# Weight pieces, loads and row statistics placed elsewhere around the stage boundaries of a two-layer kernel

## What is computed

```python
x = x + tanh(g_xattn[0]) * L0_xattn(layernorm(x), ctx)   # 16 heads of 32, int8-style projections of q and out
x = x + tanh(g_ffn[0])   * L0_ffn(layernorm(x))          # fp4 weights x fp16 group scales, 512-1408-512, silu
x = x + tanh(g_xattn[1]) * L1_xattn(layernorm(x), ctx)   # 16 heads of 128, 4 kv heads, rope, causal plus context
x = x + tanh(g_ffn[1])   * L1_ffn(layernorm(x))          # 64 experts of 512-192-512, top 8, 128 places each
```

## Time and profile before

| | us |
|---|---|
| median of 3 runs (2893.17 to 2900.97) | 2898.32 |
| profiled execution | 2892.45 |
| its span | 2890.7 |
| first attention | 0 to 508 |
| first FFN | 508 to 922 |
| projections | 922 to 1367 |
| second attention | 1367 to 2369 |
| routing | 2369 to 2483 |
| experts and last sum | 2483 to 2891 |

### The profile page before, as it was taken

The page is one execution under the profiler, slowest core; times in us unless marked ns, Lnnn a source line. Parts: engine busy times, 40 slices in busy tenths (PEclk is TensorE's granted clock), DMA queues, the critical chain, the costliest instruction groups (busy, mean ns, idle before and its releaser), DMA issues. The chain is left out here.

```text
span 2890.7 us, 48667 instructions
## 1 busy us (share of the span) xinstructions
PE 2597.6 (90%) x17291; PEld 2097.6 (73%) x17291; DVE 1703.1 (59%) x3806; ACT 1287.4 (45%) x3413; POOL 877.6 (30%) x878
## 2 busy tenths in 40 slices
PE   7899986699998899997999999999999974599895
PEld 5666753699997788885888888888888864355552
DVE  6767677944344766664766666666666656422221
ACT  4777775222223544443655555555555531122121
POOL 3344223200001555553322222222222220244443
PEclk9999998799999999998999999999999985799997
DMA  3110011400013555556412422421331127799976
GB/s 132 48 45 23 20 56 52 126 30 16 30 37 106 181 185 190 191 189 233 140 45 88 142 65 57 144 60 51 92 108 45 38 77 252 217 305 293 298 187 112
DMA packets 227215, 340.07 MB, mean 118 GB/s; under 512 B 24736, under 2 KB 111136, under 8 KB 226464
## 3 DMA queue, kind: packets, MB, share of 16 engines
q1 hardware_dynamic: 209664, 292.78, 31.7%
q0 software_dynamic: 14912, 39.85, 6.7%
q10 hardware_dynamic: 2400, 4.33, 0.5%
HBM read 230.56 MB, written 110.53 MB: 118 GB/s over the span
## 5 line engine op out<-in xcount | busy, mean ns | idle before, releaser
L2019 POOL TENSOR_SCALAR a_prob<-a_prob,a_rinv 128x640 f32<-128x640 f32 (+3 forms) x256 | 252.4, 986 | 756.9 <-DVE a_rinv L2180 756.9
L2170 DVE TENSOR_REDUCE a_mx<-a_s_ps 128x1 f32<-128x640 f32 (+3 forms) x256 | 262.3, 1025 | 250.7 <-PE a_s_ps L2090 244.8
L2043 ACT ACTIVATE a_probT<-a_t_ps 128x512 fp32r<-128x512 f32 (+3 forms) x512 | 237.0, 515 | 349.4 <-PE a_t_ps L2098 349.4
L2186 DVE TENSOR_TENSOR a_probT<-a_t_ps,a_probT 128x512 fp32r<-128x512 f32 (+3 forms) x512 | 276.8, 583 | 47.2 <-ACT a_probT L2043 47.1
L2034 ACT ACTIVATE a_prob<-a_s_ps,a_nb,a_rs 128x640 f32<-128x640 f32 (+3 forms) x256 | 267.9, 1046 | 15.7 <-DVE a_nb L2171 15.7
L137 PE MATMUL a_o_ps<-a_probT,a_v 128*128 128x256 f32 x832 | 247.1, 297 | 0.0
L138 PE MATMUL a_o_ps<-a_probT,a_v 128*128 128x256 f32 x832 | 233.6, 281 | 0.0
L139 PE MATMUL a_o_ps<-a_probT,a_v 128*128 128x256 f32 x832 | 233.5, 281 | 0.0
L2098 PE MATMUL a_t_ps<-h_ident,a_prob 128*128 128x128 f32 x1664 | 225.3, 274 | 6.7 <-DVE a_probT L2186 3.7
L2098 PEld LDWEIGHTS a_t_ps<-h_ident,a_prob 128*128 128x128 f32 x1664 | 194.6, 141 | 29.4 <-issue 3.8
L720 PE MATMUL a_bank<-a_ident,a_prob 128*128 128x128 f32 x1024 | 162.1, 287 | 39.8 <-ACT a_prob L569 30.6
(11 more groups left out here) (324 smaller groups left out, 7120.1 us busy)
## 6 DMA issues: line engine op xcount, KB each, us to landing
m_ring<-in_w_gate SPq DMA_DIRECT2D x64, 384.0 KB
m_ring<-in_w_up SPq DMA_DIRECT2D x64, 384.0 KB
m_ring<-in_w_down SPq DMA_DIRECT2D x64, 384.0 KB
l_q_hi<-p_turned SPq DMA_DIRECT2D x64, 256.0 KB, 2.4
l_q_lo<-p_turned SPq DMA_DIRECT2D x64, 256.0 KB, 2.1
h_split<-l_q_hi SPq DMA_DIRECT2D x62, 256.0 KB, 3.1
h_split<-l_q_lo SPq DMA_DIRECT2D x62, 256.0 KB, 3.8
h_x<-x SPq DMA_DIRECT2D x32, 256.0 KB, 3.2
```

The costliest lines, as they stand in the source:

```text
L2019: pool.tensor_scalar(prob[:, k % 4, 0:w], prob[:, k % 4, 0:w], rinv[:, k % 4:k % 4 + 1], 1.0, ALU.mult, ALU.mult).then_inc(s["weighted"], 1)
L2043: act.activation(probT[0][:, pair % 2, i * 4:i * 4 + n, k % 2], t_ps[i][:, 0:n * P].rearrange("p (m n) -> p m n", n=P), ACT.Copy).then_inc ...
L2170: step(dve.tensor_reduce(mx[:, k % 4:k % 4 + 1], s_ps[:, k % 2, 0:w], AX.X, ALU.max))
L2186: dve.tensor_tensor(probT[1][:, pair % 2, i * 4:i * 4 + n, k % 2], t_ps[i][:, 0:n * P].rearrange("p (m n) -> p m n", n=P), probT[0][:, pai ...
```

## The change

At the first boundary a new function `early_piece` puts the steps of pieces 0 to 4, with their low splits, into fifteen groups G = 49 to 63 on DVE; piece 6 is made at G = 64 and the low split of 5 at G = 65. ACT's six high splits stand after `copy_out` in six groups of the loop, and POOL does no split any more, in either stage. SP's loads for them come earlier, words 6 to 8 before the last store. In the FFN `norm(1, t)` stands before the pieces.

At the second, weights of the projections' tile 0 are split one chunk ahead rather than two, and in tile 0 alone the next tile's rows are turned after K_CTX and copied at V_CTX.

At the third, `first_loads` is gone: ACT loads the rows, queries 0 and 1 and keys 0 and 1, one chunk earlier, and SP loads the rest at the start of the second attention, between the pieces of wo and v, where wo 3 to 6 now also are. The splits of wo come two heads later.

At the fourth, `measure(tile)` takes mean and variance of each tile in the second attention, two heads after its `add`, into `moments`, a buffer of [128, 16, 2] that outlives the stage. The routing takes one root for all 16 tiles, loads rows straight into the token table's buffer, normalises two tiles of each batch on ACT and two on DVE, has two buffers for the turned rows, of whose copies DVE takes one in four, and another order on DVE.

The diff, its core (unchanged lines are mostly left out, twelve leading blanks are cut, and of the routing and the early pieces not all is shown):

```diff
@@ -260,6 +260,9 @@
     return ("K", b, 3) if b < 1 else ("k", b, 7)
...
+PIECES_AT = GROUPS0 - 15
@@ -384,12 +387,25 @@
             load_mask(t + 2)
+        if t == TILES - 1:
+            ffn["load_words"](sp, EARLY0)
+            ffn["load_scale"](sp, EARLY0)
...
         if t == TILES - 4:
+            ffn["load_scale"](sp, 2)
+            ffn["load_scale"](sp, 3)
+            ffn["load_words"](sp, 3)
+        if t == TILES - 3:
+            ffn["load_scale"](sp, 4)
+            ffn["load_words"](sp, 4)
+        if t == TILES - 2:
+            ffn["load_words"](sp, 5)
+            ffn["load_scale"](sp, 5)
+        if t == TILES - 5:
@@ -401,13 +417,9 @@
                 ffn["load_rows"](sp, x_out, u)
-        if t >= TILES - 2:
-            ffn["load_scale"](sp, t - (TILES - 2) + 2)
-    ffn["load_words"](sp, 3)
-    ffn["load_scale"](sp, 4)
-    ffn["load_words"](sp, 4)
-    ffn["load_words"](sp, 5)
-    ffn["load_scale"](sp, 5)
+    ffn["load_words"](sp, EARLY0 + 1)
+    ffn["load_scale"](sp, EARLY0 + 1)
+    ffn["load_words"](sp, EARLY0 + 2)
@@ -609,13 +620,20 @@
         copy_out(G - 1)
-        if G == GROUPS0:
+        if G == PIECES_AT + 2:
...
             ffn["split_high"](act, 0)
+        if G == PIECES_AT + 3:
             ffn["split_high"](act, 1)
-        if G == GROUPS0 + 1:
+        if G == PIECES_AT + 6:
             ffn["split_high"](act, 2)
+        if G == PIECES_AT + 8:
+            ffn["split_high"](act, 3)
+        if G == PIECES_AT + 11:
+            ffn["split_high"](act, 4)
+        if G == PIECES_AT + 14:
+            ffn["split_high"](act, 5)
@@ -625,8 +643,6 @@
-    for n in range(3, EARLY0):
-        ffn["split_high"](act, n)
@@ -883,6 +899,47 @@
+    def early_piece(at):
+        if at == 0:
+            ffn["left_shift"](dve, step)
+            ffn["shift_bits"](dve, step, 0)
+            ffn["mask_bits"](dve, step, 0)
+        elif at == 1:
+            ffn["scale_bits"](dve, 0)
+            ffn["shift_bits"](dve, step, 1)
+        elif at == 2:
+            ffn["mask_bits"](dve, step, 1)
+            ffn["scale_bits"](dve, 1)
+        elif at == 3:
+            ffn["split_low"](dve, 0)
+            ffn["shift_bits"](dve, step, 2)
+        elif at == 4:
+            ffn["split_low"](dve, 1)
+            ffn["mask_bits"](dve, step, 2)
...
+        elif at == 14:
+            ffn["split_low"](dve, 4)
@@ -915,16 +972,7 @@
         copy_turned(4 * G - 1)
-        if G == GROUPS0 - 10:
-            ffn["left_shift"](dve, step)
-        if GROUPS0 - 9 <= G < GROUPS0:
-            n = (G - (GROUPS0 - 9)) // 3
-            if G % 3 == (GROUPS0 - 9) % 3:
-                ffn["shift_bits"](dve, step, n)
-            elif G % 3 == (GROUPS0 - 8) % 3:
-                ffn["mask_bits"](dve, step, n)
-            else:
-                ffn["scale_bits"](dve, n)
+        early_piece(G - PIECES_AT)
@@ -944,14 +992,9 @@
                 scale_x(b + 2, 2 * (g - 11), 2 * (g - 11) + 2)
+        if G == GROUPS0:
+            ffn["make_whole"](dve, step, EARLY0)
         if G == GROUPS0 + 1:
-            for n in range(3):
-                ffn["split_low"](dve, n)
-            ffn["make_whole"](dve, step, 3)
-            ffn["make_whole"](dve, step, 4)
-            ffn["make_whole"](dve, step, 5)
-            dve.wait_ge(h["s"]["split_lo"], 4)
-            ffn["split_low"](dve, 4)
@@ -1149,7 +1193,8 @@
     sp.dma_start(gate[:], row_of(d["g_ffn"], 0, 1)).then_inc(gate_loaded, 16)
-    for n in range(EARLY0, PIECES0):
+    ffn["load_scale"](sp, EARLY0 + 2)
+    for n in range(EARLY0 + 3, PIECES0):
@@ -1188,9 +1233,6 @@
             root(m["ve"], m["rstd"], var_ready, rstd_ready, UNITS * SUB)
-        if u == 0:
-            for n in range(GU_PIECES, PIECES0):
-                ffn["split_low"](pool, n)
@@ -1352,17 +1394,14 @@
     context(0)
-    ffn["make_whole"](dve, step, EARLY0)
+    for t in range(SUB):
+        norm(1, t)
     for n in range(EARLY0, PIECES0):
-        if n + 1 < PIECES0:
+        if WHOLE0 <= n + 1 < PIECES0:
             ffn["make_whole"](dve, step, n + 1)
-        if n < GU_PIECES:
-            ffn["split_low"](dve, n)
+        ffn["split_low"](dve, n)
...
             inner(n - EARLY0 - 1)
-        if n == GU_PIECES - 1:
-            for t in range(SUB):
-                norm(1, t)
@@ -1578,17 +1617,6 @@
-    def first_loads():
-        for slot in range(RING_T):
-            sp.wait_ge(t_stored[slot], 32 * (NT * TURNED // RING_T))
-        sp.wait_ge(r_stored[0], 16)
-        sp.wait_ge(s["normed"], TILES - 1)
-        load_rows(sp, early, scr, x_src, 0)
-        sp.wait_ge(s["produced"], (TILES - 1) * CHUNKS + 2)
-        load_keys(sp, early, scr, 0, 0)
-        sp.wait_ge(s["produced"], (TILES - 1) * CHUNKS + SHARED_CH)
-        load_queries(sp, early, scr, 0)
@@ -1617,8 +1645,6 @@
                 sp.dma_start(scr["r"][g // NT, g % NT], rr[:, g % 2, 0:Q_CHUNKS]).then_inc(r_stored[g % 2], 16)
-        if ck - LAG == (TILES - 1) * CHUNKS:
-            first_loads()
@@ -1702,20 +1728,22 @@
     def next_loads(ch):
-        if ch == SHARED_CH + 1:
+        if ch == SHARED_CH:
...
                 act.wait_ge(t_stored[slot], 32 * (NT * TURNED // RING_T))
+            load_keys(act, early, scr, 0, 0)
+        elif ch == SHARED_CH + 1:
+            load_queries(act, early, scr, 0)
+            act.wait_ge(r_stored[0], 16)
+            act.wait_ge(s["normed"], TILES - 1)
+            load_rows(act, early, scr, x_src, 0)
+        elif ch == SHARED_CH + 2:
             load_keys(act, early, scr, 0, 1)
-        elif ch == SHARED_CH + 2:
+        elif ch == SHARED_CH + 3:
             load_queries(act, early, scr, 1)
-            load_keys(act, early, scr, 0, 2)
-        elif ch == SHARED_CH + 3:
-            load_queries(act, early, scr, 2)
-            load_keys(act, early, scr, 0, 3)
...
     weights["high"](act, SHARED_CH)
-    weights["high"](act, SHARED_CH + 1)
@@ -1739,10 +1767,10 @@
                 act.activation(cT[0][:], cx[:, g % 2], ACT.Copy).then_inc(s["c_hi"], 1)
-            if ch == V_SELF and g + 1 < TILES:
+            if ch == (V_SELF if g else V_CTX) and g + 1 < TILES:
                 x_hi(g + 1)
-            if ck + SHARED_CH + 2 < CHUNKS:
-                weights["high"](act, ck + SHARED_CH + 2)
+            if ck + SHARED_CH + 1 < CHUNKS:
+                weights["high"](act, ck + SHARED_CH + 1)
@@ -1792,7 +1820,7 @@
             mm.then_inc(s["produced"], 1)
-            if ch == Q_CHUNKS and g + 1 < TILES:
+            if ch == (Q_CHUNKS if g else K_CTX) and g + 1 < TILES:
@@ -1878,7 +1906,6 @@
     weights["low"](dve, SHARED_CH)
-    weights["low"](dve, SHARED_CH + 1)
@@ -1894,13 +1921,13 @@
                 scale_self(g)
-                if g + 1 < TILES:
-                    x_lo(g + 1)
...
                 scale_ctx(g)
-            if ck + SHARED_CH + 2 < CHUNKS:
-                weights["low"](dve, ck + SHARED_CH + 2)
+            if ch == (V_SELF if g else V_CTX) and g + 1 < TILES:
+                x_lo(g + 1)
+            if ck + SHARED_CH + 1 < CHUNKS:
+                weights["low"](dve, ck + SHARED_CH + 1)
@@ -1975,12 +2003,20 @@
-    sp.dma_start(gate[:], row_of(d["g_xattn"], 1, 1)).then_inc(s["gate_loaded"], 16)
...
         load_wo(h)
-    for g in range(1, G1):
-        load_v(0, g)
+    load_keys(sp, early, scr, 0, 2)
+    load_queries(sp, early, scr, 2)
+    load_wo(3)
+    load_v(0, 1)
+    load_wo(4)
+    load_keys(sp, early, scr, 0, 3)
+    load_wo(5)
+    load_v(0, 2)
+    load_wo(6)
+    load_v(0, 3)
+    sp.dma_start(gate[:], row_of(d["g_xattn"], 1, 1)).then_inc(s["gate_loaded"], 16)
@@ -1991,8 +2027,9 @@
             load_queries(sp, early, scr, quad + 3)
-        for h in range(3 + 4 * quad, min(7 + 4 * quad, H1)):
-            load_wo(h)
+        if quad:
+            for h in range(3 + 4 * quad, min(7 + 4 * quad, H1)):
+                load_wo(h)
@@ -2004,6 +2041,7 @@
                 sp.wait_ge(x_stored[(tile - 1) % 2], 16 * ((tile - 1) // 2 + 1))
+                sp.wait_ge(s["measured"], tile)
@@ -2061,9 +2099,9 @@
         exp(k + 2)
-        if k < H1:
-            weight_hi(k)
-        if k == H1:
+        if 2 <= k < H1 + 2:
+            weight_hi(k - 2)
+        if k == H1 + 2:
@@ -2205,6 +2243,11 @@
+    def measure(tile):
+        dve.wait_ge(s["added"], tile + 1)
+        step(dve.bn_stats(stats[:], x[:, tile % 2]))
+        dve.bn_aggr(moments[:, tile], stats[:]).then_inc(s["measured"], 1)
@@ -2218,9 +2261,12 @@
         most(k + AHEAD1)
+        if k % H1 == 6 and k >= H1:
+            measure(k // H1 - 1)
         invert(k + 2)
-        if k < H1:
-            weight_lo(k)
+        if 2 <= k < H1 + 2:
+            weight_lo(k - 2)
+    measure(TILES - 1)
@@ -2293,46 +2337,54 @@
+        sp.wait_ge(s["normed_act"], 2 * j + 2)
+        sp.dma_start(t_dst[ORDER[j]], tab[:, ORDER[j]]).then_inc(stored, 16)
...
+    for b in ORDER:
+        for i in range(2):
```

(58 more changed lines are left out.)

134 lines of the change are left out of this document (60 added, 74 removed).

## The result

The changed kernel takes 2876.91 us (median of 4, 2875.0 to 2882.89), the kernel before beside it 2895.74; the ratio is 0.9945, 95% interval 0.9931 to 0.9960. That is 18.8 us less, not the 41.5 forecast, and 2876.9 stands at the very edge of my range. The profiled execution takes 2882.89 us, its span is 2881.1.

The account below looks back on a forecast made before the run. PE was busy 90% of the span, so gains lay at the seams where it idles. Terms 9.2 + 2.3 + 16 + 14 = 41.5 off the profiled 2892.45 us, plus 5.87 for the median: forecast 2857, 8-in-10 range 2839 to 2877.

Parts of the forecast that it names:

- the third seam: Projections to second attention: 11 us from fewer, earlier loads plus 5 from wo; 16 us gained, bounds 8 and 20.
- the second seam: FFN to projections: PE's 8.89 us idle partly filled, then the weight chain is late; 2.3 us gained, bounds 0 and 4.5.
- the routing with the experts: Routing gains 20.5 us after late DMA, less 3.5 for gathered rows and 3 in the experts: 14, bounds 4 and 22.
- the first seam: First attention to FFN: 3.2 us gained before the FFN and 6 in its first unit; 9.2 us, bounds 3 and 13.
- the row statistics: Second attention: statistics for 15 tiles, 1 us each, hidden in DVE's idle time beside PE; cost nothing.
- The 5 us for wo: Start of second attention: ACT's 4.42 and PE's 3.71 us waits for wo gone; 5 us gained (3.7 to 6.6).
- needed from the third quad on, more than 20 us later: Start of second attention: SP's three added key and query loads, some 0.5 us each to issue, are not needed sooner.
- The hand-over: PE's last projection turn to second attention: query stores land in 2.1 to 4.5 us; 11 us gained, bounds 8 and 13.
- the price of the loop: First attention: ACT's six high splits cost 3.5 us, between nothing and 6.4, in the loop.
- 3 us for the experts: Experts: a weight stream that starts later against the experts holds them 3 us longer.
- the loop pays in full: Rival, first attention: casts cost 6.4 us, overruns 5, leaving 0.4 us of gain there; time 2866, chance 0.12.
- transfers take back the routing: Rival, routing and experts: full DMA engines leave a gain of 4 us there; time 2867, chance 0.12.

Follow-up runs that it names:

- light_before: The kernel before without loading the weights of experts 17 to 63, so its results are not the program's; span 2859.6 us (one run).
- stats_only: The kernel before with an unused buffer of 24 bytes per partition ahead of the second attention's three large buffers; 2888.77 us (one run).
- ahead6: Changed kernel with second seam as before, high splits before copy_out, fourth quad's queries before wo 3, stats behind large buffers, plus six gathers, not four; 2828.86 us.
- pad128: The kernel before with only an unused buffer of 128 bytes per partition allocated first; 2893.26 us, ratio 0.9997.
- placed: The changed kernel with moments at 256 bytes and stats allocated behind the second attention's three large buffers; 2869.93 us, ratio 0.9926.

## Why the prediction was wrong

By means over the traces every one of the five terms fell short of the 41.5 us: the third seam by 8.7 us (16 forecast, 7.3 measured), the second seam by 3.9, the routing with the experts by 3.9, the first seam by 3.2, the row statistics by 2.8.

**Third seam, 11 and 5 forecast, 8.6 and -1.3 measured (the first tile takes 79.4 us in place of 78.0 in the mean of the traces).** This is the largest miss. The 5 us for wo failed in the step "needed from the third quad on, more than 20 us later". It asked of the three loads that SP gained whether they come in time, but not who is queued behind SP's new wait at wo 3: the fourth quad's queries, for which PE waits 4.11 us. That queue is 3.1 us of the 6.3 missing; with the queries first, the wait behind DVE of 2.7 us is still there, so the gain of 5 was too high as well. The hand-over was right in kind and 2.4 us too high: stores land after 7 us, not 2.1 to 4.5, since loads of ACT still run beside them. A part of the 2.4 is the sum itself: 1349.0 + 0.6 + 0.7 + 0.5 + 2.8 with the middle of the landing times, 3.3, is 1356.9 and not 1356, so 10.1 us.

**First seam, 9.2 forecast, about 6 measured.** The step that failed is the price of the loop, 3.5 us for the six high splits. As time on ACT's path to PE it was nearly right, the waits behind five of them grew by 3.9 us. What had no term is the granted clock: the excess in the four tiles is 8.6 us, of which 6.05 are PE's own instructions running longer in four stays at the lower level. In the kernel before the window showed 1.00 there, and the sum has nothing for a fall from it. The second half of the step held: POOL's splits had slowed DVE, the masks are back at 0.69, and the FFN's first unit takes 79.1 us in place of 85.2 in the mean of the traces, 6.1 less (6 forecast). So the whole gain of the seam is there, and the 3.2 us ahead of the FFN came to nothing. The last store comes at 504.1, not 501.5; 2.9 us from there to the next stage was right, though 501.5 + 2.9 is 504.4 and I wrote 505.0.

**Second seam, 2.3 forecast, about -1.6 measured.** The step "those 8.89 us are in part filled" was true, and "what is late next is the weight chain" too; mis-sized was that one chunk's less lead holds PE three more times, 1.36, 2.99 and 2.54 us. I had carried a bound of 0 on this side and none below it, without a reason that excluded a loss.

**Statistics in the attention, 0 forecast.** Right for `measure`; the 2.8 us are the place of a 24-byte buffer, which no row before the run could show.

**Routing, 23.5 forecast, 23.1 measured** to the last keys in the pair before and after. The direction and the edits were right, but the agreement is in part luck. The count took only removed and moved instructions of DVE and its two waits for the table slot. In the kernel before, DVE also waits for PE's logits:

```profile
DVE r_nmax L2435 <- PE r_logit_ps L2372: 10.6, 2, 7.9
```

After, such waits come to 1.4 us, and in their place DVE waits 9.3 us for turned rows that it copies now; neither was in the count. And the stretch before is not one length: 72.8 to 73.4 us in three traces, 67.6 and 66.8 in light_before and stats_only, where the first batch's logits take 4.45 and 4.16 us and not 6.93, at a higher granted clock (0.50 from 2380 to 2390 us in the trace before, 1.00 from 2382.2 to 2387.2 in that of stats_only). After, it is 48.4 to 49.7 in all thirteen. By the means the gain is 21.4 us. The first gather's extra wait held better (the -3 for transfers and the 3.5 together were 6.5; measured 4.8 in the pair). The term that was too small is the last: 3 us for the experts, 6.2 in the mean of the traces (366.7 against 360.5) and 12.9 in the pair. My mechanism there, that a stream that starts late holds the experts longer, was wrong: ahead6 leaves the stream as it is and removes the wait.

**Sum.** With the means over the traces: 6 - 1.6 + 8.6 - 1.3 - 2.8 for all up to the routing, then 16.3 from the last add to the first expert (122.1 and 105.8) and -6.2 for the experts, is 19.0; the medians say 18.8. That the measured time still lies within the range, 0.1 us from its end, is owed to the width of the range and not to the sum. The rivals "the loop pays in full" and "transfers take back the routing" both came in part (6 us where the first rival says 0.4, 10.1 for the routing where the second says 4), and I had given each its chance alone; the range did not allow for all terms falling short at once.

## What to carry to other kernels

Work that is moved onto an engine which PE waits for can cost more than its length: PE's waits grew by 3.9 us here, and with the lower granted clock the four tiles took 8.6 us longer. Put it where that engine already waits, which gave back 5.1. When a load or a wait is moved on an in-order queue, ask of everything behind it, not of itself, whether it comes in time. A wait for a DMA in a stage with full DMA engines is not yet a bandwidth limit: a longer lead may remove it. Two more buffers did so here and gave 35 us, more than the whole change gained.

## What the runs showed of the hardware that I had not expected

A buffer of 24 bytes allocated ahead of three large ones slows 15 tiles of attention from 919.0 to 921.8 us, in all ten traces that have it there; 128 or 256 bytes ahead of all buffers did not (918.96 in pad128, 919.01 in placed). Which address matters I did not find.

In the FFN the same 256-column passes run at one of two paces: in unit 4, ten of them take 1.14 us in the trace before and 1.18 in the one after, by PE's timeline. In twelve of the 18 traces some units run at the slower pace, worth up to 2.9 us over the stage. The granted clock is 1.00 in both. The cause stays open.

PE's granted clock fell to the lower level for some microseconds inside a loop whose longest wait is 1.80 us; in light_before's trace it fell after waits of at most 0.86 us (clock 0.57 from 468 to 472 us), and the same loop with such waits stays at 1.00 in five other traces.

With the DMA engines full, two loads of the same size issued 0.14 us apart landed after 7.5 us from ACT's queue and 10.9 from SP's.
